# Making the first half's scatter tables in pieces between five attention batches of the second half

## What is computed

```python
x = x + jnp.tanh(g_xattn[0]) * _L0_xattn_ref(_layernorm(x, axis=-1), ctx_1024, ctx_1024, ...)
x = x + jnp.tanh(g_ffn[0]) * _L0_ffn_ref(_layernorm(x, axis=-1), ...)
```

```python
_, topk_idx = jax.lax.top_k(masked, TOP_K)
topk_w = jnp.take_along_axis(scores, topk_idx, axis=1)
topk_w = topk_w / (jnp.sum(topk_w, axis=-1, keepdims=True) + 1e-20)
topk_w = topk_w * ROUTED_SCALE
```

## Time and profile before

| what | value |
|---|---|
| median of 3 runs | 1419.44 us |
| lowest and highest run | 1414.52 and 1419.6 us |
| time of the profiled execution | 1419.17 us |
| span of its trace | 1417.3 us |
| PE busy | 1172.1 us (83%) |
| DVE busy | 873.8 us (62%) |
| ACT busy | 581.6 us (41%) |
| POOL busy | 499.1 us (35%) |
| mean granted TensorE clock | 0.914 |

### The profile page before, as it was taken

The page is one execution under the profiler, slowest core; times in us unless marked ns, Lnnn a source line. Parts: engine busy times, 40 slices in busy tenths (PEclk is TensorE's granted clock), DMA queues, the critical chain, the costliest instruction groups (busy, mean ns, idle before and its releaser), DMA issues.

```text
span 1417.3 us, 22633 instructions
## 1 busy us (share of the span) xinstructions
PE 1172.1 (83%) x6314; PEld 782.1 (55%) x6333; DVE 873.8 (62%) x2503; ACT 581.6 (41%) x993; POOL 499.1 (35%) x528
## 2 busy tenths in 40 slices
PE   4999988728999888297899688888759989749998
PEld 3666655405666554287788577777443333433443
DVE  6788875497878753661222134445578888576666
ACT  2566643215666532153555345555322222313322
POOL 0000000007777400017777777760715775000000
PEclk9999999858999998598999799999859999859999
DMA  9999200002222220157788567775201221000000
GB/s 308 340 320 332 121 1 0 0 1 75 78 78 78 75 54 0 50 170 251 249 255 260 195 203 218 222 218 172 71 16 36 61 59 44 22 0 1 8 7 15
DMA packets 102904, 165.23 MB, mean 117 GB/s; under 512 B 12703, under 2 KB 66471, under 8 KB 101929
## 3 DMA queue, kind: packets, MB, share of 16 engines
q1 hardware_dynamic: 82254, 122.77, 27.0%
q0 software_dynamic: 20608, 41.98, 9.9%
HBM read 74.52 MB, written 90.18 MB: 116 GB/s over the span
## 4 chain that ended last, share of the span: by engine, by line
PE 53%; DVE 16%; POOL 9%; issue 9%; DMA 7%; ACT 4%; SPq 1%; DVEq 1%; ACTq 0%
POOL sorted_rows L735 9%; DMA sb_A<-sorted_rows 6%; PE PS L589 5%; PE PS L600 5%; PE PS L1458 4%; PE PS L1448 4%; PE PS L1422 4%; PE PS L1441 4%; PE PS L1427 4%; PE PS L1517 3%; DVE sb_A L467 3%; PE PS L1499 2%; PE PS L1433 2%; PE PS L1492 2%; PE PS L1563 2%
## 5 line engine op out<-in xcount | busy, mean ns | idle before, releaser
L749 POOL DMA_INDIRECT sb_Y<-sorted_out,sb_POS x256 | 244.7, 956 | 155.1 <-issue 76.6
L735 POOL DMA_INDIRECT sorted_rows<-sb_XR,sb_POS x256 | 246.9, 965 | 80.4 <-issue 80.4
L1318 DVE SCALAR_TENSOR_TENSOR sb_A<-sb_A,PS 128x88 f32<-128x88 f32 x384 | 91.8, 301 | 251.4 <-ACT sb_A L875 243.2
L321 ACT ACTIVATE sb_A<-sb_A 128x512 f32<-128x512 f32 x128 | 80.6, 630 | 196.6 <-DVE sb_A L467 151.6
L1563 PE MATMUL PS<-sb_WGU,sb_A 128*128 x768 | 146.3, 336 | 11.1 <-issue 5.9
L600 PE MATMUL PS<-sb_A,sb_RT 128*128 128x512 f32 x256 | 134.5, 607 | 12.6 <-DVE sb_A L467 10.7
L459 DVE TENSOR_SCALAR sb_A<-PS,sb_VEC 128x512 f32<-128x512 f32 x128 | 95.8, 748 | 67.0 <-PE PS L589 65.1
L1563 PEld LDWEIGHTS PS<-sb_WGU,sb_A 128*128 128x128 f32 x768 | 123.0, 201 | 22.6 <-issue 19.1
L589 PE MATMUL PS<-sb_WGU,sb_RT 128*128 (+1 forms) x256 | 131.9, 602 | 0.1
L870 ACT ACTIVATE sb_A<-PS 128x512 f32<-128x512 f32 x96 | 57.3, 597 | 174.0 <-PE PS L1556 174.0
L717 POOL COPY sb_XR<-sb_ZT 128x512 f32 x8 | 4.9, 614 | 330.7 <-DVE sb_ZT L1142 330.7
(11 more groups left out here) (247 smaller groups left out, 2016.7 us busy)
## 6 DMA issues: line engine op xcount, KB each, us to landing
sorted_rows<-sb_RT SPq DMA_DIRECT2D x2, 18432.0 KB, 97.3
sb_A<-sorted_rows SPq DMA_DIRECT2D x96, 384.0 KB, 3.7
sorted_out<-sb_A SPq DMA_DIRECT2D x96, 256.0 KB
sb_WGU<-in_wgu SPq DMA_DIRECT2D x1, 5632.0 KB, 77.0
sorted_rows<-sb_XR,sb_POS POOLq DMA_INDIRECT x256
sb_Y<-sorted_out,sb_POS POOLq DMA_INDIRECT x256, 2.6
sb_RW<-in_wd SPq DMA_DIRECT2D x1, 2816.0 KB
out<-sb_X SPq DMA_DIRECT2D x8, 256.0 KB, 2.1
```

Source lines behind the costliest of these rows:

```text
L321: nc.scalar.activation(SG[e % 2], HM[e % 2], ACT.Silu, scale=ALPHA).then_inc(l_sg, 1)
L735: pool.indirect_dma_start(out=xs[c], in_=XR[:, t, :], in_offset=None, out_offset=bass.IndirectOffsetOnAxis(ap=POS[:, b * TOPK + k:b * TOPK ...
L749: pool.indirect_dma_start(out=GBUF[r][:, k * D:(k + 1) * D], out_offset=None, in_=ys[c], in_offset=bass.IndirectOffsetOnAxis(ap=POS[:, b * ...
L1318: ins = v.scalar_tensor_tensor(EH[:, t, :], ESI[:, t, :], XB[r][:, t, one(e[t] + D)], gu_bank[r % 2][:, t, EI:2 * EI], ALU.mult, ALU.mult)
```

## The change

The seven functions leave their place ahead of `queries(lo)` of half 1's attention. The first five bodies of the loop (batches 16 to 20) are written out by hand, and the functions stand between and behind them: `chosen_scores` after the first body, `weights` and `slot_counts` after the second, `slot_table` after the third, `positions` after the fourth, and `eight_positions` and `rows_of_positions` after the fifth. The loop then starts at batch 21. PE's, ACT's, POOL's and SP's programs stay as they are.

```diff
                 vn(lo)
-                if c:
-                    chosen_scores()
-                    weights()
-                    slot_counts(c - 1)
-                    slot_table(c - 1)
-                    positions()
-                    eight_positions()
-                    rows_of_positions(c - 1)
                 queries(lo)
                 keys(lo)
                 next_z(lo + 1)
...
                 if c + 1 < CHUNKS:
                     dve.wait_ge(ld_x[c + 1], 32)
-                S.loop(lo, hi - 2, body, 10 if c + 1 < CHUNKS else 9)
+                first = lo
+                if c:
+                    body(lo)
+                    chosen_scores()
+                    body(lo + 1)
+                    weights()
+                    slot_counts(c - 1)
+                    body(lo + 2)
+                    slot_table(c - 1)
+                    body(lo + 3)
+                    positions()
+                    body(lo + 4)
+                    eight_positions()
+                    rows_of_positions(c - 1)
+                    first = lo + 5
+                S.loop(first, hi - 2, body, 10 if c + 1 < CHUNKS else 9)
                 body(hi - 2, True)
```

## The result

The changed kernel takes 1435.1 us in the median of 4 runs (1425.75 to 1439.89), against 1419.52 us before (1414.52 to 1422.45). The ratio is 1.0113 with a 95% interval of 1.0073 to 1.0153, so it is slower. The forecast was 1438.9 us, and the range of 1433 to 1447 us holds the median. The profiled execution was the shortest of the four: 1425.75 us, with a span of 1423.9 us and a mean granted clock of 0.920 (before 0.914).

A forecast was written before the change was run, and what follows sets the result against it. The prediction took PE's work to bound half 1's attention. It added only the 19.7 us wait at route, not attention's 1.9 us: 1419.2 + 19.7 = 1438.9 us, range 1433 to 1447 us.

The forecast's parts named there:

- The tables: Half 1's attention: the seven functions' results are ready at 382.6 us, 65.7 us later than the 316.88 before.
- the scatter's completion: Half 0's scatter on POOL: complete at 548.3 us instead of 482.6, past its 46.1 us of slack.
- Attention was to lose 1.9 us: Half 1's attention: 6.5 us gained at the front, 8.4 us lost to PE stalls, +1.9 us by itself.
- 19.7 forecast: Start of half 1's route: waits for half 0's scatter until 548.3 us instead of starting at 528.62, costing 19.7 us.
- The "not slower" one: Rival: half 1's route does not wait for the scatter, attention alone decides, 1412.7 to 1421.1 us; chance 0.04.
- The clock rival: Rival: each of the first four PE gaps in attention drops the clock, 2.1 us each, 1447.3 us; chance 0.12.
- the first four gaps: PE in half 1's attention: stalls behind the first four pieces, 1.3, 2.6, 0.3 and 1.3 us, together 5.5.
- the fifth: PE in half 1's attention: the stall behind the fifth piece, whose next body is in the loop, 2.9 us.
- DVE did not hold up the scatter: Rival: DVE's work beside half 1's MLP slows the last 52 scatter DMAs, 5.9 us more, 1444.8 us; chance 0.03.
- The pieces: Half 1's attention: DVE work put behind five bodies, partly absorbed, stalls PE by 8.4 us in all.
- the shift stays whole: Everything behind half 1's route is chained to it, so the 19.7 us delay reaches the end in full.

The follow-up runs named there:

- Experiment 5: Changed kernel with only 64 of the 128 scatter DMAs of half 0 issued: 1417.31 us, ratio 0.9992 to the kernel before.
- experiment 12: Kernel before plus 24 useless DVE instructions (17.3 us) at the wait for the scatter in half 1's route: 1432.29 us, ratio 1.0115.
- experiments 2 to 4: Changed kernel with the seven functions spread over three, four or seven bodies instead of five: 1424.21, 1425.31 and 1457.12 us.
- experiment 2: Changed kernel with the seven functions in pieces behind the first three bodies instead of five: 1424.21 us, ratio 1.0043 to the kernel before.
- experiment 3: Changed kernel with the seven functions in pieces behind the first four bodies instead of five: 1425.31 us, ratio 1.0063 to the kernel before.
- the repeat: The changed kernel run again without any edit: 1429.13 us, ratio 1.0076 to the kernel before.
- four bodies: Same run as experiment 3: the seven functions behind the first four bodies instead of the changed kernel's five, 1425.31 us.
- seven bodies: Changed kernel with one piece each behind bodies 1, 2, 3, 4, 6 and 7: 1457.12 us, ratio 1.0265 to the kernel before.
- the padding: Same run as experiment 12: kernel before plus 24 useless DVE instructions in half 1's route, 1432.29 us.
- three bodies: Same run as experiment 2: the seven functions behind the first three bodies instead of the changed kernel's five, 1424.21 us.
- the control: Kernel before with the same 64 of 128 scatter DMAs of half 0 left out: 1418.79 us, ratio 1.0007 to the kernel before.
- experiment 7: Against the changed kernel, four functions back at the front, two in the first body, the last behind it: 1413.27 us, ratio 0.9971 to the kernel before.

## Why the prediction was right, and which term was off

**The mechanism.** Each step of it stands in the trace. The tables were forecast at 382.6 us and came at 381.56; the scatter's completion at 548.3, and route started at 547.71. Attention was to lose 1.9 us and loses 1.4 and 1.9 in two traces (190.5 and 191.0 against 189.1). The MLP and the wait together grow by 17.1 and 17.9 us, against 17.8 (19.7 - 1.9). Up to route's sigmoid the three stretches sum to 263.2 us before and to 280.9 and 282.3 after, so the change costs 17.7 and 19.1 us there, against 19.7 forecast. Experiment 5 shows that the wait is the whole of it, within 2 us, experiment 12 that such a wait alone is enough, and experiments 2 to 4 that it grows with the number of bodies.

**The rivals.** The "not slower" one had its condition right: with the wait gone, the time is that of before (0.9992, that is -4.4 to +2.0 us, which still holds the +1.9 us I gave it). In the changed kernel itself the scatter was reached. The clock rival was wrong as a whole, since the first four gaps, at most 1.78 us, leave the clock alone. It was right for the fifth, of 2.25 us, whose matmuls take 1.6 us longer, and for the gap of 4.57 us in experiment 2, but not for the equal gap of 2.25 us in experiment 3. DVE did not hold up the scatter: 1.279 against 1.276 us per DMA.

**The pieces.** The first four gaps, each with the 0.40 us behind it, are 0.9, 2.2, 0 and 0.9 us, together 4.0 against the 5.5 forecast. The fifth is 2.25 + 1.6 = 3.9 us, against 2.9, and of it the 1.6 are the clock, which I had put at nothing. The sum, 7.9, is near the 8.4 by two errors that cancel, which is luck.

**The term that was off: "the shift stays whole".** I had 19.7 us at route and 19.7 at the end. The medians give 15.6 us, and 11.2 in the repeat. That the range holds the first median is partly luck, since 7 of the 10 executions of the two measurements lie below 1433 us. Of the missing microseconds 2.0 and 0.6 are missing ahead of route's sigmoid already (17.7 and 19.1); the rest is behind it. Three other kernels keep their shift. Up to the sigmoid the traces of four bodies, seven bodies and the padding take 7, 37 and 16 us more than that of before, and their medians are 7, 39 and 16 us over before. In the two traces of the changed kernel, the choice and the experts are 6 us shorter than in the two of the kernel before, and layer 1 is 6 and 1 us shorter. The stretch at the start of the second half's experts, in the columns of the earlier trace rows, of the kernel before:

```profile
796.00:836.00 40.00, 31.05 (x176) 28.46 (x177) 12.41 (x40) 15.02 (x30) 30.24 (x33) 0.75 0.65 209
```

Of the changed kernel:

```profile
813.00:853.00 40.00, 32.18 (x216) 28.80 (x216) 15.39 (x45) 17.34 (x35) 30.25 (x33) 0.92 0.73 232
```

And of the changed kernel again:

```profile
816.00:856.00 40.00, 33.73 (x221) 29.51 (x222) 15.49 (x46) 18.34 (x37) 30.25 (x33) 0.92 0.73 232
```

In the same 40 us PE does 216 and 221 matmuls instead of 176, at a clock of 0.92 instead of 0.75. The same stretch of three bodies and of seven bodies:

```profile
806.00:846.00 40.00, 31.53 (x209) 28.21 (x210) 15.23 (x45) 17.18 (x34) 30.25 (x33) 0.90 0.72 230
840.00:880.00 40.00, 32.17 (x202) 28.97 (x203) 13.06 (x43) 16.73 (x34) 30.34 (x32) 0.84 0.70 217
```

Three bodies, with no wait at route, has the high clock and a short stage (418.9 us); seven bodies, with the longest wait, has less clock and the long stage (423.8). So the wait by itself does not make the stage shorter. The Trainium skill (TensorE: Matmul & The Clock Gate, Part 1) says that the window in which activity is watched runs freely, so that the point at which the clock rises differs between runs of one kernel. The traces agree in so far as the clock fell behind a gap of some 2.25 us in three traces (the changed kernel, its repeat, experiment 5) and held behind one in experiment 3. Executions of one kernel also differ by up to 14 us here (1425.75 to 1439.89), and the two slowest of the first four have the lowest mean clock, 0.911; that the clock's rise makes this spread is not shown. That the longer ones (1438.91 and 1439.89) sit at 19 to 20 us over before fits a shift that is whole unless the clock gives some back. Whether the change makes the early rise more likely stays open. Two traces of before with 424 us against two with 418 are for it. The bare padding's 424.5 us, the 423.8 of seven bodies and the control's 421.1 are against it.

## What to carry to other kernels

Work that is moved off a busy engine's path delays whatever waits for it. Before spreading it out, add up its delay and the length of what it starts, and set that against the slack of the next consumer: here 65 us against 46. The place for such work is a wait the engine has anyway (8.20 us and 3.80 us here, worth 3 to 4 us in experiment 7), early enough that the long transfer behind it is still hidden. Between two bodies of this loop, a piece on DVE cost PE its length less some 1.4 to 2.3 us, and in three of four traces with a gap of 2.25 us some clock on top.

## What the runs showed of the hardware

The granted clock held through gaps of 1.78 and 1.99 us. Behind a gap of 4.57 us it fell from 2.4 to 1.2 GHz for about one group of matmuls (3.78 us instead of 2.05). Behind gaps of 2.25 us it fell in three traces (3.64, 3.19 and 3.67 us for the group) and held in a fourth (2.05), so that the same gap has no fixed price. The same kernel differs by 6 to 19 us between executions on chips of the usual speed. For the kernel before the 28 executions lie between 1407.78 us at a mean clock of 0.925 and 1426.07 at 0.910, so that a change worth 0.3% needed 12 runs beside 28. And on one chip the unchanged kernel took 1907.57 us instead of 1417; the three kernels profiled there had mean clocks near 0.80 and stretches of up to 50 us without work that no instruction of the profile explains. Times from two chips could not have been compared.
